# Dense-projection inputs of an attention block: fp16 parts made token-major and transposed by DMA instead of by TensorE

## Chip, cores and metric

One core of a Trainium2 chip. The metric is the device time of one execution in microseconds (us). Engines: TensorE (PE; its weight loads are PEld), VectorE (DVE), ScalarE (ACT), GpSimd (POOL), and SyncE (SP), which issues nearly all DMAs.

## What is computed

A macaron block on x of shape (2, 1024, 512), float32: half a feed-forward network (FFN), attention, half an FFN, each on a layer-normalised input and added to x.

```python
x = x + 0.5 * ffn(layernorm(x))
x = x + attn(layernorm(x))
x = x + 0.5 * ffn(layernorm(x))
# attn: q, k, v = h @ w_qkv.T + b_qkv, 32 heads of 16, 8 k/v heads, rotary, causal softmax
ctx = jnp.einsum('bhqk,bkhd->bqhd', probs, v).reshape(B, S, HIDDEN)
out = jnp.einsum('bsh,oh->bso', ctx, w_dense) + b_dense
# ffn: W = mean + mean(|w - mean|) * sign(w - mean); (silu(x @ W1.T) * (x @ W3.T)) @ W2.T
```

The change lies in `out`, the dense projection of the attention's context.

## The kernel before

All products run on PE with operands split into two fp16 parts (high and low), three products for each (`PASSES`). Tokens are 16 row tiles of 128 (8 for each of the two sequences), and tiles are grouped by four into chunks for the FFNs.

**Attention.** There are 16 groups, one for each sequence and k/v head (group g is sequence g // 8). A loop over k (PE L2058, DVE L1621) runs scores of group k for the row maxima in 25 "pieces" (`later_piece`; DVE reduces each, L1552 and L1556) beside the transposed scores and values of groups k-1 and k-2 (`scores_t` L2012, `values` L2030; exponentials on ACT, L983; masks on POOL, L734). PSUM banks are shared: a piece needs the bank of an earlier piece, given back by DVE. `split_rowmax` (L1559) ends a group; PE transposes the maxima (L2009), ACT copies them to `mrow`, and SP writes them with four DMAs (L579) into the operands of that group, which `scores_t` waits for. `transpose_context` (PE L2055) and `normalise` (DVE L1579) then write the group's context into `context`, token-major, fp32, in SBUF.

**Dense projection.** After the loop a sequence written out by hand (PE from L2148) mixes what is left of groups 14 and 15 with row tiles 0 to 7, the first sequence's, whose context is complete since group 7. For each row tile i: `transpose_rows(i)` (PE, L2124, the transposes have line L2133) makes four 128x128 fp32 transposes into PSUM bank 4 + i % 2; `context_high` (DVE L1652, from tile 8 on ACT L1035) and `context_low` (DVE L1659) write high and low fp16 parts into `ctx_t[i % 2]`; `project(i, q)` for q = 0 to 3 (PE L2136, products have line L2143) makes 12 products into the same bank; `add_dense` (DVE L1664) adds it to x. Tiles 8 to 15 follow when the attention is over: the dense tail.

**Into the second FFN.** The statistics, the normalised rows (`both_rows` L1670), their differences and their fp16 parts (`row_hi` on ACT L1041, `row_lo` on DVE L1681) of the first FFN chunk are made beside the tiles. `place_rows` (SP L594) transposes them by DMA into `xs`, two 128x1792 transposes for each of two halves (L602). `load_pair(n)` (SP L586) loads one of 28 slices of FFN weights into four slots; the first two do not overlap the attention's memory, the others do. `pair_products` (PE L2256, products have line L2271) begins the second FFN. SP works in its program's order: a wait holds all that stands behind it.

## Time and profile before

| | |
|---|---|
| median of 3 runs | 1449.14 us (1448.33 to 1449.30) |
| profiled execution | 1450.07 us, span of its profile 1448.4 us |
| PE busy | 1374.4 us, 95% of the span |
| DVE / ACT / POOL busy | 1066.3 (74%) / 608.2 (42%) / 182.7 us (13%) |
| DMA moved | 144.40 MB, mean 100 GB/s |
| chain that ended last | PE 77%, DVE 13%, SP's queue 3% |

All times of rows are microseconds from the start of the span of one profiled execution; its own time is 0.93 us above the median. A row names a line of the kernel, an engine, an operation and out<-in tiles. Matmuls are pipelined, so a busy PE is not PE at its peak. Of SP the rows show how long an issue held its queue, and the DMA view how long it took until the data landed. The granted clock of PE is given as a share of 2.4 GHz.

### The profile page before, as it was taken

The page shows a single profiled execution, that of the slowest core. Times are in us where ns is not written, and L with a number is a line of the kernel's source. Part 1 is how long each engine was busy: PE and PEld are TensorE (multiplying, and loading weights), DVE is VectorE, ACT ScalarE, POOL GpSimd, SP SyncE. Part 2 cuts the span into 40 slices and gives each one's busy share as a digit, 9 for nine tenths or more (in the row PEclk, how much of TensorE's full clock was granted, in tenths as well). Part 3 has the DMA queues.
Part 4 walks back from the last instruction along what each step waited for, and adds up shares of the span by engine and source line. Part 5 has one row for each costly group of instructions (what it writes and reads, how often), then busy time and mean ns, then how long its engine had stood idle before and what let it go on. Part 6 is the DMA issues. An engine that isn't in the chain of part 4 may idle for free.

```text
span 1448.4 us, 25511 instructions
## 1 busy us (share of the span) xinstructions
PE 1374.4 (95%) x9984; PEld 706.9 (49%) x9984; DVE 1066.3 (74%) x1611; ACT 608.2 (42%) x802; POOL 182.7 (13%) x269
## 2 busy tenths in 40 slices
PE   1999999999999978799999999999999999999998
PEld 0444444444444433233333333333577777777775
DVE  7999566764665578899999999965576666665544
ACT  4862222222211243378787777765222222222121
POOL 0000000000000354133323222211011011011000
PEclk9999999999999999699999999999999999999999
DMA  9703941011021021111111111030635646566540
GB/s 386 256 0 108 258 133 58 26 57 48 31 46 40 1 59 30 52 28 28 26 36 27 28 26 38 2 132 1 182 116 173 215 168 220 159 226 182 197 160 30
DMA packets 152028, 144.40 MB, mean 100 GB/s; under 512 B 129904, under 2 KB 133488, under 8 KB 148080
## 3 DMA queue, kind: packets, MB, share of 16 engines
q1 hardware_dynamic: 151920, 142.91, 31.4%
q8 instruction: 73, 1.20, 0.3%
q14 instruction: 35, 0.29, 0.1%
HBM read 96.73 MB, written 21.76 MB: 82 GB/s over the span
## 4 chain that ended last, share of the span: by engine, by line
PE 77%; DVE 13%; SPq 3%; issue 3%; ACT 3%; DMA 1%; POOL 0%; ACTq 0%; DVEq 0%
PE ps L2271 17%; PE ps L1819 15%; PE ps L2288 10%; PE ps L2045 9%; PE ps L1946 6%; PE ps L1840 6%; PE ps L2026 4%; PE ps L1866 3%; PE ps L2143 2%; PE ps L1936 2%; SPq L528 2%; SPq L532 2%; DVE rowmax L1552 1%; DVE w_raw L1167 1%; PE ps L2055 1%
## 5 line engine op out<-in xcount | busy, mean ns | idle before, releaser
L983 ACT ACTIVATE probs<-ps 128x1024 f32<-128x1024 f32 (+3 forms) x384 | 292.5, 812 | 83.9 <-PE ps L2026 82.3
L1819 PE MATMUL ps<-xt_hi,w_all 128*128 128x512 f16 x896 | 275.9, 382 | 16.2 <-DVE w_all L1207 16.0
L2271 PE MATMUL ps<-xs,wpair 128*128 128x256 f16 x2352 | 261.3, 273 | 0.9 <-DVE second_sum L1704 0.9
L2271 PEld LDWEIGHTS ps<-xs,wpair 128*128 128x128 f16 x2352 | 229.9, 98 | 33.7 <-DVE second_sum L1704 1.1
L1552 DVE TENSOR_REDUCE rowmax<-ps 128x2 f32<-128x1024 f32 (+3 forms) x208 | 237.3, 1141 | 9.0 <-PE ps L1954 3.8
L1946 PE MATMUL ps<-ka,qa 48*128 48x512 f16 (+3 forms) x768 | 159.7, 342 | 22.3 <-DVE rowmax L1552 9.5
L1819 PE MATMUL ps<-xt_lo,w_all 128*128 128x512 f16 x448 | 171.1, 382 | 0.0
L2045 PE MATMUL ps<-probs,vs 128*32 128x512 f32 (+3 forms) x1536 | 164.5, 500 | 2.4 <-ACT ctx_sb L1002 2.4
L1819 PEld LDWEIGHTS ps<-xt_hi,w_all 128*128 (+1 forms) x896 | 88.0, 98 | 124.9 <-issue 18.6
L1556 DVE TENSOR_REDUCE rowmax<-ps 128x1 f32<-128x512 f32 x192 | 131.1, 683 | 9.8 <-PE ps L1946 9.8
L2288 PE MATMUL ps<-wpair,hs_hi 128*128 128x512 f16 x448 | 133.4, 380 | 0.5 <-DVE hs_lo L1731 0.5
L2026 PE MATMUL ps<-qa,ka 50*128 50x512 f16 (+3 forms) x768 | 131.7, 331 | 1.7 <-DMA qa<-mrow 1.0
L1064 ACT ACTIVATE both<-both,scal 128x1024 f32<-128x1024 f32 x28 | 32.1, 1148 | 221.1 <-DVE both L1704 221.1
L734 POOL TENSOR_SCALAR_AFFINE_SELECT probs<-probs 128x512 f32<-128x512 f32 x128 | 81.2, 634 | 317.4 <-ACT probs L983 317.4
L1946 PEld LDWEIGHTS ps<-ka,qa 48*128 48x128 f16 x768 | 48.7, 95 | 139.6 <-DVE rowmax L1552 69.5
L1840 PE MATMUL ps<-w_all,hhia 128*128 (+1 forms) x336 | 100.0, 380 | 1.1 <-DVE x L1379 1.1
L1362 DVE SCALAR_TENSOR_TENSOR ha<-ps,scal,silua 128x512 f32<-128x512 f32 x42 | 31.5, 750 | 88.3 <-PE ps L1819 67.2
L2288 PE MATMUL ps<-wpair,hs_lo 128*128 128x512 f16 x224 | 85.0, 380 | 0.0
L2026 PEld LDWEIGHTS ps<-qa,ka 50*128 50x128 f16 x768 | 40.1, 94 | 67.7 <-ACT probs L983 44.5
L1819 PEld LDWEIGHTS ps<-xt_lo,w_all 128*128 (+1 forms) x448 | 44.0, 98 | 52.9 <-issue 1.1
L703 POOL TENSOR_TENSOR rot_s<-qkv_raw,sin 128x320 f32<-128x320 f32 x32 | 35.5, 1128 | 267.7 <-ACT qkv_raw L959 250.2
L910 ACT CAST hhia<-ha 128x512 f16<-128x512 f32 x42 | 25.9, 618 | 102.1 <-DVE ha L1362 102.1
(168 smaller groups left out, 1818.1 us busy)
## 6 DMA issues: line engine op xcount, KB each, us to landing
wpair<-spill SPq DMA_DIRECT2D x28, 2304.0 KB, 8.9
spill<-block_parts SPq DMA_DIRECT2D x14, 512.0 KB, 2.7
spill<-w_all SPq DMA_DIRECT2D x24, 224.0 KB, 4.0
x<-x_in SPq DMA_DIRECT2D x4, 1024.0 KB, 5.5
wbase<-m1t SPq DMA_DIRECT2D x4, 896.0 KB, 12.4
w_raw<-w1t SPq DMA_DIRECT2D x4, 896.0 KB, 13.9
wbase<-m3t SPq DMA_DIRECT2D x4, 896.0 KB, 24.0
w_raw<-w3t SPq DMA_DIRECT2D x4, 896.0 KB, 24.2
```

The lines of the kernel that those rows point to most:

```text
L734: nc.gpsimd.affine_select(out=p, in_=p, compare_op=ALU.is_ge, fill=0.0, base=0, pattern=[[0, Q_PER_KV], [1, P]], channel_multiplier=-1).th ...
L983: nc.scalar.activation(probs[u % PBUF][:, 2 * pair:2 * pair + 2, 0:q1 - q0], wide(("scores", g, (u, pair)))[:, :, 0:q1 - q0], ACT.Exp, sca ...
L1552: nc.vector.tensor_reduce(dst, src, AX.X, ALU.max).then_inc(pair_taken, 1)
L1556: nc.vector.tensor_reduce(rowmax[:, slot, kind, j:j + 1], ps[:, SINGLE_BANK, 0:w], AX.X, ALU.max)\
L1819: last = mm(ps[:, bank, :], w[a][:, k, bass.ts(t, P)], xt[b][:, k, :], start=(k == 0 and n == 0), stop=(k == HB - 1 and n == 2))
L1840: last = mm(ps[:, DOWN + j, :], hs[a][:, j * P:(j + 1) * P], w[b][:, t, :], start=(first and n == 0), stop=(last_tile and n == 2))
L1866: last = mm(ps[:, DOWN + j, :], first_split(t, a)[:, j * P:(j + 1) * P], w2s[b][:, t, :], start=(t == 0 and n == 0), stop=(t == IT - 1 and ...
L1946: return mm(ps[:, bank, off:off + w], qa[g % BUF][64 * b:64 * b + ROWS, j, qt * P:(qt + 1) * P], ka[g // 2 % BUF][64 * b:64 * b + ROWS, k0 ...
L2026: last = mm(bank[:, b, 0:q1 - q0], ka[g // 2 % BUF][64 * b:64 * b + MROWS, kt * P:(kt + 1) * P], qa[v][64 * b:64 * b + MROWS, pair, q0:q1] ...
L2045: last = mm(ps[32 * h:32 * h + 32, CTX_BANK, at:512], vs[g // 2 * 2 % BUF + h % 2][:, kt, :], probs[u % PBUF][:, h, 0:q1 - q0], start=firs ...
L2271: last = mm(product_bank(n, i)[:, m, :], weight_of(n, m, a, weight, k), xs[c % 2][:, b, 2 * rows_ + k, :], start=(k == 0 and q == 0), stop ...
L2288: last = mm(ps[:, DOWN + j, :], hs2[n % 2][a][:, q, j * P:(j + 1) * P], down_weight(n, b, q), start=(p == 0 and q == 0 and i == 0), stop=( ...
```

## The change

`transpose_rows` goes from PE. The high and low fp16 parts of the context are made token-major from `context` into three buffers `ctx_parts`, and SP transposes each part by DMA (128x512, two for each tile) into one of now four buffers `ctx_t`. The first two tiles are made inside DVE's loop over groups, in its last round. In SP's program the first two pair loads move from behind the last group's row-maximum transfers to behind those of group 14.

In order: buffers and helpers; SP (`place_context`, the loop over groups, behind it); ACT; DVE (parts, the loop over groups, behind it); PE. `project` keeps its place in PE's sequence, and the other calls of `transpose_rows` go as the last one does.

```diff
     wd_all = at("wd_all", [P, 2, HB, HID], F16, R0)
     wd = [wd_all[:, i, :, :] for i in range(2)]
     bd = at("bd", [P, HID], F32, R0 + 8192)
-    ctx_t = [[at(f"ctx_t{n}{i}", [P, HB, P], F16, R0 + 10240 + i * 2048 + j * 1024) for j, n in enumerate(("hi", "lo"))]
-             for i in range(2)]
+    ctx_t = [[at(f"ctx_t{n}{i}", [P, HB, P], F16, a + j * 1024) for j, n in enumerate(("hi", "lo"))]
+             for i, a in enumerate((R0 + 10240, R0 + 12288, D0 + 14336, C0 + 6144))]
+    ctx_parts = [at(f"ctx_parts{i}", [P, 2, HID], F16, B0 + 45056 + i * 2048) for i in range(3)]
     assert R0 + 14336 == D0
     PAIR_COLS = 2 * 3584 + 2048
...
         return {5: xt5, 6: xt6}.get(n) or (xt0 if n % 2 == 0 else xt1)
     LN_AT = {4: 4, 8: 5, 12: 6}
+    def ctx_parts_free(eng, i):
+        if i >= 3:
+            eng.wait_ge(ctx_placed[(i - 3) % 4], 32 * ((i - 3) // 4 + 1))
+    def context_rows(i):
+        return context[:, i % SEQ_TILES, :, i // SEQ_TILES, :]
+    def context_ready(eng, i):
+        b, tt = divmod(i, SEQ_TILES)
+        eng.wait_ge(single_taken, taken(("ctx", GROUPS * (b + 1) // BATCH - 1, tt // 4)))
     BLOCK_AT = {(1 if n < 8 else 2, 4 + n % 8): n for n in range(2 * HALF)}
     ON_PE = (0, 1)
...
         sp.dma_start(wd_all[:, :, :, :].rearrange("p s a b -> p (s a b)"), spill_d.ap()).then_inc(dense_loaded, 16)
         sp.dma_start(bd[:, :], b_d.partition_broadcast(P)).then_inc(dense_loaded, 16)
+        def place_context(i):
+            sp.wait_ge(ctx_hi_ready, i + 1)
+            sp.wait_ge(ctx_lo_ready, i + 1)
+            if i >= 4:
+                sp.wait_ge(dense_full, i - 3)
+            for n in range(2):
+                sp.dma_start_transpose(ctx_t[i % 4][n][:, :, :], ctx_parts[i % 3][:, n, :]).then_inc(ctx_placed[i % 4], 16)
+        def load_pair(n):
+            if n >= PAIRS:
+                return
+            if n >= WSLOTS:
+                sp.wait_ge(down2_full, n - WSLOTS + 1)
+            sp.dma_start(wpair[n % WSLOTS][:, :], image[:, n % HALF, :]).then_inc(pair_loaded[n % WSLOTS], 16)
         for g in range(GROUPS):
+            if g == GROUPS - 1:
+                place_context(0)
+                place_context(1)
             sp.wait_ge(wide_taken, drained(("rowmax", g, 0)))
             for n in range(4):
                 i, b = divmod(n, 2)
...
             if 1 <= g < GROUPS - 3:
                 sp.wait_ge(st_full, 2 * NU * g)
                 place_operands(g + 3)
-        def load_pair(n):
-            if n >= PAIRS:
-                return
-            if n >= WSLOTS:
-                sp.wait_ge(down2_full, n - WSLOTS + 1)
-            sp.dma_start(wpair[n % WSLOTS][:, :], image[:, n % HALF, :]).then_inc(pair_loaded[n % WSLOTS], 16)
+            if g == GROUPS - 2:
+                sp.wait_ge(spilled, 16 * 28)
+                for i in range(2):
+                    sp.wait_ge(blocks_spilled[i], 16 * HALF)
+                for v in range(BUF):
+                    sp.wait_ge(qk_placed[v], placed(GROUPS - BUF + v))
+                load_pair(0)
+                load_pair(1)
         def place_rows(n, j):
...
                 sp.dma_start_transpose(xs[n % 2][:, i, :, j * P:(j + 1) * P], row_parts[:, i, :])\
                     .then_inc(xs_placed[n % 2], 16)
-        sp.wait_ge(spilled, 16 * 28)
-        for i in range(2):
-            sp.wait_ge(blocks_spilled[i], 16 * HALF)
         sp.wait_ge(m_placed, 64 * GROUPS)
-        for v in range(BUF):
-            sp.wait_ge(qk_placed[v], placed(GROUPS - BUF + v))
-        load_pair(0)
-        load_pair(1)
+        for i in range(2, SEQ_TILES + 2):
+            place_context(i)
         sp.wait_ge(st_full, 2 * NU * (GROUPS - 2))
         place_rows(8, 0)
+        for i in range(SEQ_TILES + 2, SEQ_TILES + 5):
+            place_context(i)
         place_rows(8, 1)
+        for i in range(SEQ_TILES + 5, TOKEN_TILES):
+            place_context(i)
         sp.wait_ge(pv_full, NU * GROUPS)
         sp.wait_ge(single_taken, len(TURN))
         load_pair(2)
         load_pair(3)
-        sp.wait_ge(dt_full, TOKEN_TILES)
+        sp.wait_ge(dense_full, TOKEN_TILES)
         def store_rows(c):
...
         def context_high(i):
-            act.wait_ge(dt_full, i + 1)
-            act.wait_ge(dense_full, i - 1)
-            nc.scalar.copy(ctx_t[i % 2][0][:, :, :].rearrange("p a b -> p (a b)"), ps[:, rows_bank(i), :])\
+            context_ready(act, i)
+            ctx_parts_free(act, i)
+            if i == SEQ_TILES:
+                act.wait_ge(ctx_hi_ready, SEQ_TILES)
+            nc.scalar.copy(ctx_parts[i % 3][:, 0, :].rearrange("p (a b) -> p a b", a=HB), context_rows(i))\
                 .then_inc(ctx_hi_ready, 1)
         def row_hi(n, j):
...
         for i in range(SEQ_TILES, TOKEN_TILES):
             context_high(i)
-            if i in (SEQ_TILES, SEQ_TILES + 2):
-                row_hi(8, (i - SEQ_TILES) // 2)
+            if i == SEQ_TILES + 1:
+                row_hi(8, 0)
+            if i == SEQ_TILES + 4:
+                row_hi(8, 1)
         for n in range(PAIRS):
             c, p = divmod(n, HALF)
             take_first(n)
...
             if k or r >= EARLY_TAKEN:
                 reduce_piece(k, r)
+        def context_high(i):
+            context_ready(dve, i)
+            ctx_parts_free(dve, i)
+            nc.vector.tensor_copy(ctx_parts[i % 3][:, 0, :].rearrange("p (a b) -> p a b", a=HB), context_rows(i))\
+                .then_inc(ctx_hi_ready, 1)
+        def context_low(i):
+            dve.wait_ge(ctx_hi_ready, i + 1)
+            hi, lo = (ctx_parts[i % 3][:, n, :].rearrange("p (a b) -> p a b", a=HB) for n in range(2))
+            nc.vector.tensor_tensor(out=lo, in0=context_rows(i), in1=hi, op=ALU.subtract).then_inc(ctx_lo_ready, 1)
+        def context_both(i):
+            context_high(i)
+            context_low(i)
         for k in range(GROUPS):
             later_piece(k, 0)
             later_piece(k, 1)
...
             later_piece(k, 14)
             later_piece(k, 15)
             later_piece(k, 16)
+            if k == GROUPS - 1:
+                context_both(0)
             later_piece(k, 17)
             later_piece(k, 18)
             later_piece(k, 19)
             later_piece(k, 20)
+            if k == GROUPS - 1:
+                context_both(1)
             later_piece(k, 21)
             later_piece(k, 22)
             later_piece(k, 23)
...
             if ahead and p in (3, 5):
                 row_lo(9 + c, (p - 3) // 2)
-        context_high(0)
-        context_low(0)
-        context_high(1)
-        context_low(1)
+        def add_and_sum(i):
+            add_dense(i)
+            if i < TPC:
+                dve.wait_ge(x2_ready, i + 1)
+                norm_rows(8, i)
+        context_both(2)
         dve.wait_ge(wd_unit, 1)
-        add_dense(0)
-        dve.wait_ge(x2_ready, 1)
-        norm_rows(8, 0)
-        context_high(2)
-        context_low(2)
-        add_dense(1)
-        dve.wait_ge(x2_ready, 2)
-        norm_rows(8, 1)
+        add_and_sum(0)
+        context_both(3)
+        add_and_sum(1)
         normalise(14, 0)
-        context_high(3)
-        context_low(3)
-        add_dense(2)
-        dve.wait_ge(x2_ready, 3)
-        norm_rows(8, 2)
-        context_high(4)
-        context_low(4)
-        add_dense(3)
-        dve.wait_ge(x2_ready, 4)
-        norm_rows(8, 3)
+        context_both(4)
+        add_and_sum(2)
+        context_both(5)
+        add_and_sum(3)
         normalise(14, 1)
-        context_high(5)
-        context_low(5)
+        context_both(6)
         add_dense(4)
         norm_seed(8)
         norm_newton(8)
-        context_high(6)
-        context_low(6)
+        context_both(7)
         add_dense(5)
         both_rows(8, 0)
         row_differences(dve, nc.vector, 8, 0)
-        context_high(7)
-        context_low(7)
         normalise(15, 0)
         add_dense(6)
         normalise(15, 1)
         context_low(SEQ_TILES)
+        context_low(SEQ_TILES + 1)
         add_dense(7)
         row_lo(8, 0)
         for i in range(SEQ_TILES, TOKEN_TILES):
-            if i + 1 < TOKEN_TILES:
-                context_low(i + 1)
+            if i + 2 < TOKEN_TILES:
+                context_low(i + 2)
             add_dense(i)
             if i == SEQ_TILES:
                 both_rows(8, 1)
...
             later_piece(k, 24)
             values(k - 1, 4)
-        def transpose_rows(i):
-            b, tt = divmod(i, SEQ_TILES)
-            if tt % 4 == 0:
-                pe.wait_ge(single_taken, taken(("ctx", GROUPS * (b + 1) // BATCH - 1, tt // 4)))
-            if i == 0:
-                pe.wait_ge(pair_taken, NPAIR * GROUPS)
-            elif i >= 2:
-                pe.wait_ge(x2_ready, i - 1)
-            for q in range(HB):
-                last = tr(ps[:, rows_bank(i), q * P:(q + 1) * P], context[:, tt, q, b, :], ident[:, :])
-            last.then_inc(dt_full, 1)
         def project(i, q):
             if i == 0 and q == 0:
                 pe.wait_ge(dense_loaded, 32)
             if q == 0:
-                pe.wait_ge(ctx_hi_ready, i + 1)
-                pe.wait_ge(ctx_lo_ready, i + 1)
+                pe.wait_ge(ctx_placed[i % 4], 32 * (i // 4 + 1))
+                if i == 0:
+                    pe.wait_ge(pair_taken, NPAIR * GROUPS)
+                elif i >= 2:
+                    pe.wait_ge(x2_ready, i - 1)
             for n, (a, b) in enumerate(PASSES):
-                last = mm(ps[:, rows_bank(i), :], ctx_t[i % 2][a][:, q, :], wd[b][:, q, :], start=(q == 0 and n == 0),
+                last = mm(ps[:, rows_bank(i), :], ctx_t[i % 4][a][:, q, :], wd[b][:, q, :], start=(q == 0 and n == 0),
                           stop=(q == HB - 1 and n == 2))
             if q == HB - 1:
                 last.then_inc(dense_full, 1)
...
         project(7, 0)
         transpose_context(15, 1)
         project(7, 1)
-        transpose_rows(8)
         project(7, 2)
         project(7, 3)
         for i in range(SEQ_TILES, TOKEN_TILES):
-            project(i, 0)
-            if i + 1 < TOKEN_TILES:
-                transpose_rows(i + 1)
-            for q in range(1, HB):
+            for q in range(HB):
                 project(i, q)
         def pair_products(n):
```

## Rows read from the trace of the kernel before

**Rows 1.** The page: engines busy, and the granted clock of the 40 slices.
```profile
PE 1374.4 (95%) x9984; PEld 706.9 (49%) x9984; DVE 1066.3 (74%) x1611; ACT 608.2 (42%) x802; POOL 182.7 (13%) x269
...
PEclk9999999999999999699999999999999999999999
```

**Rows 2.** Windows: busy us of PE, PEld, DVE, ACT, POOL; PEclk, DMA share, GB/s.
```profile
959.00:1006.00 47.00, 46.51 (x316) 16.00 (x316) 24.17 (x52) 27.17 (x36) 6.40 (x11) 1.00 0.25 102
...
1013.00:1041.44 28.44, 25.27 (x126) 11.89 (x126) 16.86 (x24) 6.71 (x9) 0.00 (x0) 1.00 0.64 178
```

**Rows 3.** Timeline, PE, last group: start us, us, engine line op, [idle before <-releaser].
```profile
954.03 0.34 PE L1946 MATMUL ps<-ka,qa 48*128 48x384 f16 x2
```

**Rows 4.** Timeline, DVE, same stretch.
```profile
953.01 0.96 DVE L1552 TENSOR_REDUCE rowmax<-ps 128x2 f32<-128x768 f32 x1
```

**Rows 5.** Timeline, PE, first and second row transposes, first projection.
```profile
959.30 0.66 PE L2133 MATMUL ps<-ident,context 128*128 128x128 f32 x4
...
959.89 0.23 PE L2026 MATMUL ps<-qa,ka 50*128 50x128 f16 x2
...
961.56 0.59 PE L2143 MATMUL ps<-wd_all,ctx_thi 128*128 128x512 f16 x2 [0.49 <-DVE ctx_tlo L1662]
```

**Rows 6.** DVE groups by shape: count | busy us, mean ns | idle before.
```profile
L1145 DVE CAST xnorm<-xtemp 128x512 f16<-128x512 f32 x24 | 10.2, 427 | 0.8
...
L1147 DVE TENSOR_TENSOR xnorm<-xtemp,xnorm 128x512 f16<-128x512 f32 x24 | 16.6, 693 | 0.8
```

**Rows 7.** Timeline, SP: row-maximum transfers of group 14, first pair loads.
```profile
935.78 2.70 SPq L579 DMA_DIRECT2D qa<-mrow  x3
...
963.17 0.83 SPq L592 DMA_DIRECT2D wpair<-spill  x2
```

**Rows 8.** DMA issues, us to landing; second and third of windows 1000:1060, 960:985.
```profile
xt_lo<-xnorm SPq DMA_TRANSPOSE x24, 2.5
...
xs<-row_parts SPq DMA_TRANSPOSE x4, 4.3
...
wpair<-spill SPq DMA_DIRECT2D x2, 2304.0 KB, 11.5
```

**Rows 9.** Timeline, SP issues: time in which the queue is held.
```profile
514.71 1.27 SPq L499 DMA_TRANSPOSE xt_lo<-xnorm  x1
...
581.08 10.20 SPq L528 DMA_TRANSPOSE qa<-parts_q  x8
...
648.18 11.22 SPq L528 DMA_TRANSPOSE qa<-parts_q  x8
...
1016.19 3.53 SPq L602 DMA_TRANSPOSE xs<-row_parts  x2
...
1027.97 3.69 SPq L602 DMA_TRANSPOSE xs<-row_parts  x2
```

**Rows 10.** Timeline, PE, end of the attention and the dense tail.
```profile
1008.84 0.61 PE L2143 MATMUL ps<-wd_all,ctx_thi 128*128 128x512 f16 x2
...
1038.85 0.38 PE L2143 MATMUL ps<-wd_all,ctx_thi 128*128 128x512 f16 x1
...
1041.44 15.88 PE L2271 MATMUL ps<-xs,wpair 128*128 128x256 f16 x144
```

**Rows 11.** Timeline, DVE, end of the attention and the tail.
```profile
1011.07 0.42 DVE L1592 TENSOR_TENSOR context<-ps,rec 128x256 f32<-128x256 f32 x1
...
1013.16 0.75 DVE L1667 SCALAR_TENSOR_TENSOR x<-ps,scal,x 128x512 f32<-128x512 f32 x1
...
1014.07 2.03 DVE L1684 TENSOR_TENSOR row_parts<-rows,row_parts 128x1792 f16<-128x1792 f32 x1 [0.15 <-ACT row_parts L1047]
```

**Rows 12.** PE after its longest idle of the attention; windows as in rows 2.
```profile
538.54 0.61 PE L1946 MATMUL ps<-ka,qa 48*128 48x512 f16 x1 [5.02 <-DMA ka<-parts_k]
...
538.20:545.20 7.00, 6.66 (x41) 3.24 (x42) 3.74 (x5) 2.45 (x4) 2.77 (x3) 0.51 0.24 49
...
576.00:606.00 30.00, 18.77 (x130) 6.83 (x132) 24.87 (x33) 6.88 (x9) 2.30 (x6) 0.50 0.21 62
```

23 lines of the change are left out of this document (3 added, 20 removed).

## The prediction

> **What bounds the kernel now.** I read the page first: TensorE is busy for 95% of the span, at the full clock in all 40 slices but one [rows 1]. So a microsecond taken off PE's program is worth up to one microsecond, and one put in front of it costs one. The question is then what PE waits for in the three stretches that the change touches.
>
> The windows give the second reading [rows 2]. From 959 to 1006 us, where attention groups 14 and 15 are mixed with the projections of row tiles 0 to 7, PE is busy 46.5 of 47.0 us and VectorE only 24.2: there PE alone sets the pace. From 1013 to 1041.4 us, the dense tail (tiles 8 to 15), PE is busy 25.3 of 28.4.
>
> The third is the timeline of the last group of the score loop. PE starts the pair piece at 954.03 just after VectorE ends an earlier piece (953.01 + 0.96 = 953.97) [rows 3, 4]; the seven other pieces between 949 and 957 us stand the same way. So in this loop PE hands VectorE a piece at the moment at which VectorE gives a bank back. VectorE has no idle time there, and what is inserted on it moves both engines.
>
> **Part 1, transposes off PE.** One set of four holds PE from 959.30 to 959.89, 0.59 us [rows 5]. Eight such sets (tiles 0 to 7) lie in the mixed stretch; one of them took 0.49, so I take 4.6 us in all. The wait of 0.49 us ahead of the first projection [rows 5] goes too, since its tile will be ready long before. Both are on the path: -5.1 us at the end of attention. In the tail eight more sets and 3.1 us of idle time [rows 2] go, but whether this counts depends on what feeds PE there (part 3).
>
> **Part 2, two context tiles put into VectorE's last score group.** Each is a copy to fp16 (0.427 us, the nearest row is the copy of the normalised rows, same shape and same SBUF source) and a subtraction (0.693) [rows 6]. Two tiles make 2.24 us, inserted where VectorE is the tight one: +2.2 us for both engines, as rows 3 and 4 show no slack to hide it in. The lower bound is 0 (PE catches up completely), the upper 2.6 with hand-offs. The tiles 2 to 7 are copied where VectorE has half its time free [rows 2] and cost nothing; without that cover it would be 1.1 us each. ScalarE's eight copies replace eight of like size.
>
> **The moved weight loads.** The first two pair loads now start behind the row-maximum transfers of group 14, whose issues began at 935.78, so at about 938 instead of 963.17 [rows 7], and land 11.5 us after their issue [rows 8], by about 950. The first context transposes are issued at about 951, the row-maximum transfers of group 15 at about 962; neither queues behind the loads. If they did, the score rows of group 15 would wait for them. They are needed only at the start of the second FFN: 0 us. Loads two and three start after the last context transpose, seven us later than now, and are needed only when the FFN has worked off two of its 28 pairs: 0 us.
>
> **Part 3, the transposes on SP's queue.** A 128x512 transpose holds SP for 1.27 us [rows 9], and groups of eight of the operands' transposes, which are half as wide, held it for 10.20 and 11.22 us, that is 1.28 to 1.40 each. It lands 2.5 us after its issue [rows 8]. A tile needs two (high and low part): SP is held for 2.5 us, and the tile is in place 3.75 us after the first issue. In the mixed stretch eight projections fill 47 us [rows 2], one every 6 us, so this is hidden. Tile 2 stands behind the row-maximum transfers of group 15 (issued at about 962, landed by 966) and is in place by 970; projections 0 and 1 start at 961 and take until 973. If it came later, PE would wait with all of group 15 behind it, microsecond for microsecond.
>
> In the tail a projection takes PE only 1041.44 - 1038.85 = 2.59 us [rows 10], nearly the same as SP's 2.5. And in the same queue stand the two pairs of FFN row transposes, which held SP for 3.53 and 3.69 us [rows 9]. PE would be fed by SP there. Step by step, with everything at the end of attention shifted by -5.1 + 2.2 = -2.9 us:
> - Before, the projection step at 1008.84 [rows 10] was followed by the last normalisation, over at 1011.07 + 0.42 = 1011.49 [rows 11]. Now it is over at 1008.6, then comes tile 8's low part (0.69): 1009.3. PE has nothing left to project from about 1009.7.
> - SP: tiles 8 and 9 until 1014.4; the first pair of FFN rows (3.6) until 1018.0; it lands 4.3 us after its second issue [rows 8], by 1020.6, so it does not delay tile 10, which lands at +3.75, 1021.8. PE waits 3.6 us for tile 8 and 3.5 for tile 10.
> - Tile 10 is projected (2.6), VectorE adds it (0.75) and makes the second low rows (2.03) [rows 11], 0.2 for hand-offs: 1027.4. SP stood waiting for just these, with tiles 13 to 15 behind them.
> - Second pair of rows (3.65): 1031.05. Tiles 13, 14 and 15: 2.5 + 2.5 + 3.75: 1039.8, with a PE wait of 5.2 us ahead of tile 13. The last projection ends at 1042.4.
>
> Before, the FFN began at 1041.44 [rows 10]: +1.0 us. Twelve transposes of this chain at 1.35 instead of 1.25 us add 1.2, which I take because all groups of eight were slower than a single one: **+2.2 us** (bounds: +1.0, and +3.5 with each hand-off 0.1 longer).
>
> **Part 4, the clock.** PE's one long idle of the attention, 5.02 us before 538.54, was followed by the lower of the two clock levels (0.51 granted, 1.2 GHz) over the next 7 us, although PE was busy in them; and a stretch of 30 us with PE busy 63% ran at 0.50 throughout [rows 12]. The tail would have a wait of 5.2 us and be busy for 21 of 33 us. I take one fall at the wait ahead of tile 13: some 6.3 us at half speed lose 3.1 us, since PE has nothing to spare after it. Bounds: 0, and 12 for a whole tail at half speed. The last three projections would take 5.2 us each there.
>
> Sum: -5.1 + 2.2 for the attention, then the SP chain, to **+2.2** at the FFN's start, and **+3.1** for the clock: +5.3 us. The FFN behind it is bound by PE and keeps the shift. The profiled execution took 1450.07 us (span 1448.4 and 1.7 around it), 0.93 above the median; it would give 1455.4, the median 1449.14 + 5.3 = 1454.4.
>
> **Rivals.**
> - No fall of the clock, or one that SP's pace hides: +2.2, 1451.3 us (0.4 to 3.5 around it). For it: the waits of 3.5 us are followed by SP-bound tiles. Against it: [rows 12].
> - The clock falls more than once or stays low: a fall at tile 10 lengthens its projection by 2.6 us, on the chain; the whole tail low gives 8 to 12. 1457 to 1461 us. For it: the 30 us at 0.50.
> - **Faster: SP keeps ahead of PE.** If issuing a transpose cost SP little, only the first wait of 3.6 us would be left, and eight projections of 2.59: 1009.7 + 3.6 + 20.7 = 1034.0, that is -7.4 us, 1441.7. It decides at SP's share of the chain: without a fall of the clock, SP's part must be 5.1 us shorter than I have it to bring the kernel 2.9 us below the present time. Against it: every row of [rows 9]. The Trainium skill ("DMA: Bandwidth & Descriptors", section "Issuing engines are not separate DMA queues") says that a sequencer's time to initiate a DMA is usually small beside the transfer. By that rule this rival's time would come out; the trace does not agree, with 1.27 us of holding in 2.5 us to landing.
> - The change does not act, since transposes land late anyway and PE waits already in the mixed stretch: each such wait is bounded by 3.75 us; nothing in the 6 us per tile speaks for it. It lies in the slow part of the range.
>
> The skill also has a rule against this change ("VectorE: DVE Perf Modes", section "The three transpose paths"): a 128x128 transpose takes 390 ns on TensorE and 1309 ns by DMA. The trace has 0.59 us for four on PE against 3.75 for the same rows by DMA in two parts. By durations alone that is a loss for every tile; I let it stand only where PE waits, in the tail.
>
> **Numbers.** Forecast, SP chain with one fall of the clock (+3 to +7): 0.42. Without it: 0.27. Several falls: 0.15. SP ahead or a large part of VectorE's 2.2 us absorbed: 0.16. A measurement of this kernel can tell about 0.2%, 2.9 us. Faster by more than that: 0.13. Within: nearly the whole second case, the lowest of the first and some of the fourth, 0.31. Slower: 0.56. The range 1445 to 1461 leaves out most of the fast case and the end of the several falls.
>
> **What would show it.** No PE rows of the transposes, and no idle ahead of projections 0 to 7. The last score group of VectorE longer by 2.2 us. The last attention product ending about 2.9 us earlier. SP held almost without a gap from 1009 to 1038, PE waits of some 3.6, 3.5 and 5 us ahead of tiles 8, 10 and 13, released by DMA. The FFN starting near 1043 to 1047, and a granted clock under 1.00 between 1013 and 1047. The prediction is wrong if the FFN starts before 1039, if the waits sit elsewhere, or if the FFN itself changes its length, 407 us from 1041.44 to the span's end.

## The result, and the profile after

| | before | after |
|---|---|---|
| median of 20 runs | 1449.3 us | 1455.7 us |
| range | 1448.33 to 1456.88 | 1453.62 to 1457.0 |
| profiled execution (span) | 1450.07 (1448.4) | 1456.42 (1454.7) |
| second FFN begins | 1041.44 | 1047.77 |
| from there to the span's end | 407.0 | 406.9 |

The changed kernel is slower: ratio 1.0035, 95% interval 1.0027 to 1.0043, that is 3.9 to 6.2 us of 1449.3; the two medians are 6.4 us apart. The forecast was 1454.4 in a range of 1445 to 1461. All of the difference stands before the second FFN, whose length did not change.

The page of the changed kernel, engines and granted clock, answers to [rows 1]:

```profile
PE 1370.1 (94%) x9920; PEld 701.3 (48%) x9920; DVE 1063.3 (73%) x1611; ACT 607.6 (42%) x802; POOL 182.8 (13%) x269
...
PEclk8999999999999999699999999999899999999999
```

PE has 64 instructions and 4.3 us of work less, and the kernel takes longer. Two more slices now have a clock below nine tenths: the first, which lies ahead of all that was changed (it is low in some traces of unchanged code and high in others), and the one of the dense tail.

**A common zero for the traces.** Two executions of unchanged code differ by some tenths of a microsecond by the time they reach the change. One product stands ahead of everything on PE that the change moves in time, and every trace has it with the same idle ahead of it. (The moved loads are issued some 4 us before it, which is why they get an experiment of their own.) The timeline of PE has it in before and after:

```profile
942.74 0.39 PE L1946 MATMUL ps<-ka,qa 48*128 48x512 f16 x1 [0.17 <-DVE rowmax L1556]
```

```profile
942.38 0.39 PE L1982 MATMUL ps<-ka,qa 48*128 48x512 f16 x1 [0.17 <-DVE rowmax L1596]
```

I call it the marker. From it to the FFN's start it took 98.70 us before (1041.44 - 942.74) and 105.39 after, a difference of 6.69. This distance is given for every experiment below, since it leaves out what happens elsewhere in a run.

**The last score group.** PE's timeline in before and in after, at the transpose of the row maxima that ends the group:

```profile
958.91 0.24 PE L2009 MATMUL ps<-ident,nm 128*64 128x128 f16 x1
```

```profile
951.62 0.34 PE L1982 MATMUL ps<-ka,qa 48*128 48x384 f16 x2 [0.86 <-DVE rowmax L1592]
...
955.62 0.34 PE L1982 MATMUL ps<-ka,qa 48*128 48x384 f16 x2 [0.97 <-DVE rowmax L1592]
...
960.51 0.24 PE L2045 MATMUL ps<-ident,nm 128*64 128x128 f16 x1
...
962.21 0.60 PE L2170 MATMUL ps<-wd_all,ctx_thi 128*128 128x512 f16 x2
...
1005.32 0.61 PE L2170 MATMUL ps<-wd_all,ctx_thi 128*128 128x512 f16 x2
```

From the marker to that transpose it took 16.17 us before and 18.13 after: +1.96. PE waits twice for a bank, 0.86 and 0.97 us, and these answer to [rows 3, 4]. VectorE, same stretch, the first of the two tiles:

```profile
949.28 0.42 DVE L1664 CAST ctx_parts<-context 128x512 f16<-128x512 f32 x1
949.73 0.69 DVE L1670 TENSOR_TENSOR ctx_parts<-context,ctx_parts 128x512 f16<-128x512 f32 x1
```

The first projection (962.21) waits for nothing, where [rows 5] had 0.49 us. The product that answers to the 1008.84 of [rows 10] starts at 1005.32: 62.94 us from the marker instead of 66.10, that is -3.16. The last score group cost 1.96 of it, so the transposes taken off PE gave 5.12.

**The tail.** PE's waits there, and the start of the FFN:

```profile
1012.43 1.03 PE L2170 MATMUL ps<-wd_all,ctx_thi 128*128 128x512 f16 x2 [3.25 <-DMA ctx_tlo<-ctx_parts]
...
1021.96 0.74 PE L2170 MATMUL ps<-wd_all,ctx_thi 128*128 128x512 f16 x2 [2.69 <-DMA ctx_tlo<-ctx_parts]
...
1037.30 1.03 PE L2170 MATMUL ps<-wd_all,ctx_thi 128*128 128x512 f16 x2 [5.71 <-DMA ctx_tlo<-ctx_parts]
...
1047.77 12.50 PE L2286 MATMUL ps<-xs,wpair 128*128 128x256 f16 x113
```

SP's timeline over the same stretch: both parts of tile 8, the first pair of row transposes, the low parts of tiles 10 and 12, the second pair of row transposes, and the low part of tile 13 (answers to [rows 9]):

```profile
1008.65 1.19 SPq L598 DMA_TRANSPOSE ctx_thi<-ctx_parts  x1
1009.88 1.27 SPq L598 DMA_TRANSPOSE ctx_tlo<-ctx_parts  x1
...
1013.87 3.51 SPq L639 DMA_TRANSPOSE xs<-row_parts  x2
...
1019.44 1.27 SPq L598 DMA_TRANSPOSE ctx_tlo<-ctx_parts  x1
...
1024.68 1.27 SPq L598 DMA_TRANSPOSE ctx_tlo<-ctx_parts  x1
1029.21 3.50 SPq L639 DMA_TRANSPOSE xs<-row_parts  x2
...
1034.77 1.27 SPq L598 DMA_TRANSPOSE ctx_tlo<-ctx_parts  x1
```

Each wait of PE ends 2.5 us after the low part of its tile was issued (1009.88 to 1012.43, 1019.44 to 1021.96, 1034.77 to 1037.30). From 1025.95 (1024.68 + 1.27) to 1029.21 SP stands idle: it waits for the second low rows, and the transposes of tiles 13 to 15 stand behind them. VectorE shows why these rows come late, since they follow the addition of tile 10 (answers to [rows 11]):

```profile
1026.45 0.75 DVE L1714 SCALAR_TENSOR_TENSOR x<-ps,scal,x 128x512 f32<-128x512 f32 x1 [4.62 <-PE ps L2170]
1027.12 2.02 DVE L1731 TENSOR_TENSOR row_parts<-rows,row_parts 128x1792 f16<-128x1792 f32 x1
```

Tile 10 kept PE from 1021.96 to the addition at 1026.45, 4.5 us where the prediction had 2.6. The windows of the same execution (busy us of PE, PEld, DVE, ACT, POOL; PEclk, DMA share, GB/s) give the reason:

```profile
1012.10:1015.50 3.40, 3.07 (x8) 1.13 (x9) 0.40 (x1) 1.06 (x2) 0.00 (x0) 0.50 0.51 103
1022.30:1025.70 3.40, 3.40 (x10) 1.22 (x8) 0.00 (x0) 0.93 (x2) 0.00 (x0) 0.50 0.49 99
1036.00:1042.80 6.80, 5.50 (x13) 1.94 (x14) 0.16 (x1) 0.00 (x0) 0.00 (x0) 0.50 0.66 98
```

The clock fell to its lower level (0.50 granted, 1.2 GHz) at all three waits: 0.4 us before the end of the wait ahead of tile 8, 0.3 us into tile 10, and 1.3 us before the end of the wait ahead of tile 13. The first fall is hidden: tiles 8 and 9 run slowly while SP is behind anyway. The second delays the addition of tile 10, and with it SP. The third makes the last three projections take 10.47 us (1037.30 to 1047.77) instead of the 7.8 of full speed.

### The profile page after: what moved, and what is told of

It reads as the page before. It is cut to its first block, busy times and chain, and to the rows that moved or that the text cites. A ratio compares the mean times of both kernels' runs of the same rounds, so it can differ in the third digit from the quotient of the medians.

```text
span 1454.7 us, 25424 instructions
## 1 busy us (share of the span) xinstructions
PE 1370.1 (94%) x9920; PEld 701.3 (48%) x9920; DVE 1063.3 (73%) x1611; ACT 607.6 (42%) x802; POOL 182.8 (13%) x269
## 4 chain that ended last, share of the span: by engine, by line
PE 76%; DVE 13%; issue 3%; SPq 3%; ACT 3%; DMA 1%; POOL 0%; ACTq 0%; DVEq 0%
PE ps L2286 17%; PE ps L1855 14%; PE ps L2303 10%; PE ps L2081 9%; PE ps L1982 6%; PE ps L1876 6%; PE ps L2062 5%; PE ps L1902 3%; PE ps L2170 2%; DVE rowmax L1592 2%; PE ps L1972 2%; PE ps L2091 1%; DVE w_raw L1207 1%; DVE rowmax L1596 1%; SPq L545 1%
```

## Experiments

Theory: SP's queue sets the tail, issue after issue, and the falls of the clock in PE's waits come on top; the two tiles in VectorE's last score group cost about 2 us on the path; the moved pair loads cost nothing. Rivals: the moved loads or what queues behind them; the row transposes in the queue rather than the number of issues; the work given to VectorE in the tail. Here is what all kernels gave. The ratio is to the kernel before, run beside each of them (its medians were 1449.2 to 1449.5). Times and distances do not carry the same weight: the distance is one execution of each kernel, and the intervals of waits_filled, second_rows_last and pair_on_gpsimd overlap that of the changed kernel, so that for these three a gain over the changed kernel rests on the distance and on the medians, and is not clear of the noise by the ratio.

| kernel | median us (runs) | ratio (95%) | marker to FFN |
|---|---|---|---|
| before | 1449.3 (20) | | 98.70 |
| after | 1455.7 (20) | 1.0035 (1.0027 to 1.0043) | 105.39 |
| loads_moved | 1450.02 (10) | 1.0002 (0.9992 to 1.0012) | 98.70 |
| loads_back | 1463.78 (4) | 1.0102 (1.0085 to 1.0119) | 112.22 |
| waits_filled | 1453.63 (6) | 1.0029 (1.0016 to 1.0041) | 101.42 |
| second_rows_last | 1453.29 (7) | 1.0037 (1.0020 to 1.0054) | 100.62 |
| pair_behind_loop | 1457.46 (4) | 1.0070 (1.0047 to 1.0092) | 103.56 |
| pair_on_gpsimd | 1453.88 (6) | 1.0025 (1.0013 to 1.0038) | 103.48 |
| rows_out_of_tail | 1445.90 (11) | 0.9978 (0.9969 to 0.9988) | 94.69 |
| rows_and_pair | 1443.43 (5) | 0.9958 (0.9944 to 0.9972) | 92.31 |
| one_transpose | 1450.30 (10) | 0.9997 (0.9984 to 1.0011) | 99.65 |
| all_three | 1438.76 (5) | 0.9929 (0.9915 to 0.9942) | 88.23 |

### The pair loads

**loads_moved**: the kernel before, with nothing but the move of the first two pair loads.

```diff
         for g in range(GROUPS):
...
                 place_operands(g + 3)
+            if g == GROUPS - 2:
+                sp.wait_ge(spilled, 16 * 28)
...
+                load_pair(0)
+                load_pair(1)
...
         sp.wait_ge(m_placed, 64 * GROUPS)
...
-        load_pair(0)
-        load_pair(1)
         sp.wait_ge(st_full, 2 * NU * (GROUPS - 2))
```

> The kernel before with one part of the change alone: the first two pair loads issued behind the row-maximum transfers of group 14. Theory (SP's queue feeds the dense tail): the loads cost and bring nothing, 1449.3 us, FFN start within 0.5 us of 1041.4. Rival (the early loads disturb attention's last group through the DMA engines): 1 to 3 us slower, with longer waits of PE or SP between 938 and 960 us.

The distance from the marker to the FFN is the one of before to the hundredth, 98.70. The move alone costs nothing and brings nothing.

**loads_back**: the changed kernel, with the two loads where they stood before, so that the transposes of tiles 2 to 9 are issued behind them.

```diff
         sp.wait_ge(m_placed, 64 * GROUPS)
...
+        load_pair(0)
+        load_pair(1)
         for i in range(2, SEQ_TILES + 2):
             place_context(i)
```

> The changed kernel with the first two pair loads back behind the row-maximum transfers of group 15. Theory: the transposes of tiles 2 and on then stand behind 4.6 MB of loads; they land 10 to 12 us later, at about 978 instead of 970, and PE waits for tile 2 (3 to 6 us) if the DMA engines serve SP's queue in order: 1459 to 1461 us. Rival (the loads are the harm of the change): the attention gets faster than in the changed kernel, 1453 us or less.

SP's timeline behind the loads, then PE's:

```profile
965.47 0.83 SPq L606 DMA_DIRECT2D wpair<-spill  x2
966.41 1.31 SPq L598 DMA_TRANSPOSE ctx_thi<-ctx_parts  x1
967.76 1.29 SPq L598 DMA_TRANSPOSE ctx_tlo<-ctx_parts  x1
969.16 7.54 SPq L598 DMA_TRANSPOSE ctx_thi<-ctx_parts  x1
976.76 2.41 SPq L598 DMA_TRANSPOSE ctx_tlo<-ctx_parts  x1
```

```profile
980.34 1.04 PE L2169 MATMUL ps<-wd_all,ctx_thi 128*128 128x512 f16 x2 [6.96 <-DMA ctx_tlo<-ctx_parts]
```

Two transposes behind the loads are issued at the usual pace; the third holds SP for 7.54 us and the fourth for 2.41, until the second load is in (issued at 965.9, landed 13.3 us later). PE then waits 6.96 us in the middle of the attention, and the FFN starts 6.83 us later than in the changed kernel (112.22 against 105.39). The direction was as expected and the size above it. So the move of the loads is needed with this change, and it is what keeps it from costing 14 us.

### What the clock costs

**waits_filled**: the changed kernel; PE makes 12, 10 and 20 products into a free bank ahead of tiles 8, 10 and 13. They are added to the work, and their results go nowhere.

```diff
+        pe.wait_ge(wide_taken, len(WIDE))
         for i in range(SEQ_TILES, TOKEN_TILES):
+            for n in range({SEQ_TILES: 12, SEQ_TILES + 2: 10, SEQ_TILES + 5: 20}.get(i, 0)):
+                mm(ps[:, 2, :], ident16[:, :], wd[0][:, 0, :], start=True, stop=True)
```

> The changed kernel with PE kept busy in its three waits of the tail by products whose result nobody reads: 12 ahead of tile 8, 10 ahead of tile 10, 20 ahead of tile 13 (of 0.216 us each, less than the waits of 3.25, 2.69 and 5.71 us). It computes the same result. Theory: the clock stays at 1.00 in the tail, the projection of tile 10 takes 2.6 us instead of 4.3 and tiles 13 to 15 7.8 instead of 10.5: FFN start 4.4 us earlier, at about 1043.4, 1451.3 us. Rival (the waits alone make the loss, the clock only follows): same time as the changed kernel within 1 us.

PE's timeline in the tail, and the window over it:

```profile
1008.24 2.75 PE L2270 MATMUL ps<-wd_all,ident 128*128 128x512 f16 x12
...
1016.86 2.32 PE L2270 MATMUL ps<-wd_all,ident 128*128 128x512 f16 x10
...
1029.03 4.48 PE L2270 MATMUL ps<-wd_all,ident 128*128 128x512 f16 x20
...
1035.22 0.61 PE L2170 MATMUL ps<-wd_all,ctx_thi 128*128 128x512 f16 x2 [1.71 <-DMA ctx_tlo<-ctx_parts]
...
1043.04 15.23 PE L2289 MATMUL ps<-xs,wpair 128*128 128x256 f16 x138
```

```profile
1008.24:1043.04 34.80, 30.45 (x140) 12.85 (x139) 15.90 (x23) 4.95 (x7) 0.00 (x0) 1.00 0.67 139
```

No fall is left, and with work that serves nothing this execution is shorter. The distance is 101.42: 3.97 us less than in the changed kernel and 2.72 more than before. That parts the loss in two. The SP chain without any fall of the clock costs +2.7; the falls cost 4.0, of which 1.7 on SP's chain (the second rows are issued 85.10 us after the marker instead of 86.83) and 2.65 on the last three projections (7.82 instead of 10.47), less 0.4 that the second row transposes held SP longer. In the medians the gain is smaller, 2.1 us (1455.7 to 1453.63), with the six runs from 1451.46 to 1455.4; by the two ratios it is 0.9 us, inside the noise. Each run's mean granted clock is on record: 0.987 in the two shortest, 1451.46 and 1451.67, and 0.980 to 0.985 in the other four, so the clock may have fallen somewhere in these all the same. One profile can't say where. The clock's part is 4 us in the profiled pair and some 2 us, or less, over the runs.

### The row transposes in SP's queue

**second_rows_last**: only SP's order is changed; the second row transposes go behind tile 15.

```diff
         place_rows(8, 0)
-        for i in range(SEQ_TILES + 2, SEQ_TILES + 5):
+        for i in range(SEQ_TILES + 2, TOKEN_TILES):
             place_context(i)
         place_rows(8, 1)
-        for i in range(SEQ_TILES + 5, TOKEN_TILES):
-            place_context(i)
```

> The changed kernel with the second pair of FFN row transposes issued behind tile 15 instead of between tiles 12 and 13. Theory (tiles 13 to 15 wait in SP's queue behind these rows, which wait for tile 10): the wait ahead of tile 13 goes, SP ends tile 15 at about 1034, the rows land at about 1040.5, and the FFN starts there: 7 us faster than the changed kernel, 1448.5 us. Rival (VectorE's added copies and the first two waits make the loss): the wait only moves to another tile, less than 2 us faster.

SP's timeline, VectorE's, and PE's at the start of the FFN:

```profile
1024.22 1.27 SPq L598 DMA_TRANSPOSE ctx_tlo<-ctx_parts  x1
1027.65 1.19 SPq L598 DMA_TRANSPOSE ctx_thi<-ctx_parts  x1
```

```profile
1024.97 2.02 DVE L1729 TENSOR_TENSOR row_parts<-rows,row_parts 128x1792 f16<-128x1792 f32 x1
1026.91 0.68 DVE L1668 TENSOR_TENSOR ctx_parts<-context,ctx_parts 128x512 f16<-128x512 f32 x1
```

```profile
1042.55 15.88 PE L2284 MATMUL ps<-xs,wpair 128*128 128x256 f16 x144 [1.06 <-DMA xs<-row_parts]
```

The rows no longer hold tile 13 in the queue, but its low part is made behind the low rows on VectorE, so SP stands idle all the same from 1025.49 to 1027.65. The distance is 100.62. Against the kernel with filled waits, the fair comparison since here too no fall delays the end, the new order is worth only 0.8 us in the distance, and the ratio shows no gain (1.0037). The expectation of 7 us was missed, and its rival, that the wait only moves to another tile, came nearer (PE waits 1.89 us ahead of tile 13 and 1.94 ahead of tile 15): two queues, VectorE's and SP's, held tile 13, and I had taken it out of one. The row transposes, now last, cost PE time in two ways: the low part of tile 15, with them right behind it in the queue, takes 4.6 us from issue to landing instead of 2.5, and the FFN's start waits 1.06 us for them.

This trace also says something of the clock. Up to tile 12 it runs the same program as the changed kernel, with the same wait of 3.25 us ahead of tile 8; but the clock fell only 1.1 us into that tile (0.50 from 1013.1 to 1016.5) and did not fall at all behind the wait of 2.48 us ahead of tile 10, where the changed kernel lost 1.7 us behind 2.69. So how much the falls cost differs from one execution to the next.

**rows_out_of_tail**: the statistics come right behind tile 3, and the first rows, with their transposes, inside the attention. Tile 8 is made on VectorE right behind its normalisation, the high part of the first rows moves from ScalarE to VectorE, and the second rows come last. The diff shows SP and the core of VectorE.

```diff
-        for i in range(2, SEQ_TILES + 2):
+        for i in range(2, SEQ_TILES):
             place_context(i)
...
         place_rows(8, 0)
-        for i in range(SEQ_TILES + 2, SEQ_TILES + 5):
+        for i in range(SEQ_TILES, TOKEN_TILES):
             place_context(i)
         place_rows(8, 1)
-        for i in range(SEQ_TILES + 5, TOKEN_TILES):
-            place_context(i)
...
         add_and_sum(3)
+        norm_seed(8)
+        norm_newton(8)
...
         normalise(15, 0)
+        context_both(SEQ_TILES)
         add_dense(6)
...
             if i == SEQ_TILES:
-                both_rows(8, 1)
-                row_differences(dve, nc.vector, 8, 1)
-            if i == SEQ_TILES + 2:
                 row_lo(8, 1)
```

> The changed kernel with SP's tail left to the context tiles: statistics of the first FFN chunk right behind tile 3, first row parts made and transposed inside the attention, second row transposes behind tile 15, and tile 8 made by VectorE alone right behind the normalisation it needs. Theory (SP's chain sets the tail): tile 8 in place at about 1010.1, tiles 2.6 us apart, last projection over at 1031, row transposes landed at 1033.6, where the FFN starts: 14 us faster than the changed kernel, 1441.5 us, and 8 faster than the kernel before. Rival (the DMA transposes are slower than PE's in themselves, whatever else is in the queue): the tiles come more than 3.4 us apart, as before the change, and the FFN starts later than 1040.

The median is 1445.9, 3.2 us under the kernel before by the ratio, and the distance 94.69, 10.7 less than in the changed kernel. The profiled execution itself was 1452.61, the highest of the eleven: the clock had fallen at 850.3 us, to 0.50 until 857.1, long before this stretch, which the distance from the marker leaves out. PE's waits are 1.02 to 1.59 us each, and the clock does not fall in the tail. The order of nearly the same work, with as many transposes, was worth more than the whole loss. It came out some 4 us above what was expected: all of PE's waits ahead of a tile are still released by the transpose of a low part, and the FFN's first product waits 1.32 us for the row transposes. The kernel rows_and_pair below has the same order, and its trace shows what holds the low parts: SP stands idle from 1010.02 to 1011.55 and from 1014.06 to 1015.33, until VectorE, busy with the second rows, has made them (1010.80 + 0.69 and 1014.58 + 0.69).

### The pair in the last score group

**pair_behind_loop**: tiles 0 and 1 are made behind VectorE's loop instead of in it.

```diff
             later_piece(k, 16)
-            if k == GROUPS - 1:
-                context_both(0)
...
+        context_both(0)
+        context_both(1)
         context_both(2)
```

> The changed kernel with the parts of tiles 0 and 1 made by VectorE behind its loop over groups instead of inside its last round. Theory (2.0 us of copies stand on the path inside the loop): the last row-maximum transpose of PE comes 2.0 us earlier (at about 958.5 instead of 960.5), without the waits of 0.86 and 0.97 us on VectorE; but tile 0 is in place only at about 962.7, PE waits 2.5 us for it, and the FFN starts 0 to 1 us later than in the changed kernel: 1456.0 us. Rival (PE has slack for the pair in the loop): the transpose stays near 960.5 and the wait for tile 0 is added in full, 1458 us.

PE's timeline:

```profile
958.50 0.24 PE L2043 MATMUL ps<-ident,nm 128*64 128x128 f16 x1
...
963.11 0.59 PE L2168 MATMUL ps<-wd_all,ctx_thi 128*128 128x512 f16 x2 [2.85 <-issue]
```

The transpose of the maxima is 16.17 us behind the marker (958.50 - 942.33), as before the change: the pair accounts for the 1.96 us, all of it. But now PE waits 2.85 us for tile 0, and the product that answers to 1005.32 starts 63.88 us behind the marker, 0.94 later than in the changed kernel, as expected. The distance to the FFN is 1.83 shorter all the same: in this execution, the shortest of the four, the clock stayed low longer in tiles 8 to 10 (0.50 from 1012.5 to 1019.4) and did not fall at tile 10, which PE then waited for only 1.19 us. The four runs lie between 1454.52 and 1463.37, so the time says little more than that the place is no better.

**pair_on_gpsimd**: the same two tiles on GpSimd, which has nothing to do for 8 us there.

```diff
         for k in range(GROUPS + 2):
...
+            if k == GROUPS - 1:
+                context_pair(0)
+                context_pair(1)
...
             later_piece(k, 16)
-            if k == GROUPS - 1:
-                context_both(0)
```

> The changed kernel with the parts of tiles 0 and 1 made by GpSimd in a stretch where it idles for 8 us (after 938 us). Theory: VectorE's last round is 2.0 us shorter, nothing waits for tile 0, and the whole rest moves by 2.0 us: FFN start 1045.8, 1453.7 us. Rival (GpSimd's copies from SBUF slow VectorE or delay the masks): less than 1 us gained.

GpSimd's timeline, first tile, and PE's:

```profile
937.04 0.61 POOL L781 CAST ctx_parts<-context 128x512 f16<-128x512 f32 x1
937.73 1.16 POOL L783 TENSOR_TENSOR ctx_parts<-context,ctx_parts 128x512 f16<-128x512 f32 x1
```

```profile
957.67 0.24 PE L2054 MATMUL ps<-ident,nm 128*64 128x128 f16 x1
```

Again 16.17 us behind the marker (957.67 - 941.50), and no wait for tile 0. The distance falls by 1.91 and the median by 1.8 (the ratio by 1.4 us, with overlapping intervals): VectorE's 1.96 us, passed on to the end as expected. GpSimd needs 0.61 and 1.16 us where VectorE needs 0.42 and 0.69, which costs nothing since nobody waits for it.

**rows_and_pair**: the last two kernels together (rows_out_of_tail with tiles 0 and 1 on GpSimd).

```diff
             place_context(i)
...
+            if k == GROUPS - 1:
+                context_pair(0)
+                context_pair(1)
```

> The two together (row transposes out of the tail, and tiles 0 and 1 on GpSimd). Theory: both gains add, since they lie on the path one behind the other: FFN start at 1031.6, 1439.5 us. Rival: the shorter attention leaves VectorE too little time for the row parts and tile 8, so that less than 1 us of GpSimd's 2 is left.

1443.43 us, 2.5 under rows_out_of_tail, and the distance is 2.38 less. The two gains add. The time expected, 1439.5, was missed by the same 4 us as in rows_out_of_tail.

### The number of issues

**one_transpose**: the changed kernel, with one transpose of 1024 columns for each tile instead of two of 512. Bytes and order are as they were; the buffers of a tile's two parts become one tile, and the waits count one transfer instead of two.

```diff
-            for n in range(2):
-                sp.dma_start_transpose(ctx_t[i % 4][n][:, :, :], ctx_parts[i % 3][:, n, :]).then_inc(ctx_placed[i % 4], 16)
+            sp.dma_start_transpose(ctx_both[i % 4][:, :, :, :].rearrange("p n q c -> p (n q) c"),
+                                   ctx_parts[i % 3][:, :, :].rearrange("p n h -> p (n h)")).then_inc(ctx_placed[i % 4], 16)
```

> The changed kernel with one DMA transpose of 128x1024 for each context tile instead of two of 128x512, into the same place. Theory (SP's time for each issue, not the moving of the data, sets the pace): the issue holds SP for 1.3 to 1.75 us, between the rows for 512 and for 1792 columns, instead of 2.5 for the two; tile 10 lands 2 to 2.5 us earlier, the first row transposes then wait for VectorE, and the FFN starts at about 1045 instead of 1047.8: 1452.8 us. Rival (the transfer itself is the cost): one issue of 1024 columns holds SP as long as two of 512 and lands no earlier: same time as the changed kernel within 1 us.

All issues of one line, in the changed kernel and in this one (min/median/max ns that an issue held the queue), and the time to landing:

```profile
L598 SPq DMA_TRANSPOSE ctx_thi<-ctx_parts x16: 1189/1199/1911, 950.5 to 1038.8; - x16
L598 SPq DMA_TRANSPOSE ctx_tlo<-ctx_parts x16: 1198/1267/2283, 951.8 to 1040.0; - x16
```

```profile
L597 SPq DMA_TRANSPOSE ctx_t<-ctx_parts x16: 1232/1244/2077, 949.7 to 1031.3; - x16
...
DMA to landing us min/median/max: 3.0/3.1/4.4
```

This is the clearest of the experiments. A transpose of 1024 columns holds SP for 1.24 us, one of 512 for 1.20 to 1.27. Between these two sizes the cost is that of the issue, not of the columns (the row transposes, with 1792 columns, hold it for 1.75 each). A tile takes SP 1.25 us instead of 2.5 and is in place 3.1 us after its issue instead of 3.75. The changed kernel with this one edit is level with the kernel before (0.9997, 0.9984 to 1.0011), 5.4 us under the changed kernel; the distance is 5.74 less. It was better than expected, because the wait ahead of tile 10 shrank to 0.16 us and there was no fall of the clock there; the falls at tiles 8 and 13 remain (0.50 at 1012 to 1014 and at 1032 to 1035). As second_rows_last shows, the fall at tile 10 can be missing by chance too, so some of the 5.74 may be luck.

**all_three**: rows_and_pair with one transpose for each tile. The low parts are made three tiles ahead, and the second rows are placed behind tile 13.

```diff
         place_rows(8, 0)
-        for i in range(SEQ_TILES, TOKEN_TILES):
+        for i in range(SEQ_TILES, SEQ_TILES + 6):
             place_context(i)
         place_rows(8, 1)
+        for i in range(SEQ_TILES + 6, TOKEN_TILES):
+            place_context(i)
...
-            if i + 2 < TOKEN_TILES:
-                context_low(i + 2)
+            if i + 3 < TOKEN_TILES:
+                context_low(i + 3)
```

> Row transposes out of the tail, tiles 0 and 1 on GpSimd, one transpose for each tile; in addition the context parts are made three tiles ahead on VectorE and the second row transposes stand behind tile 13. Theory: tile 8 lands at about 1008, PE then has a tile at hand every 2.6 us, and the FFN starts at 1029 to 1030 instead of 1035.1 in the kernel with the first two edits: 1437.5 us, 12 us faster than the kernel before. Rival (another wait takes the place: VectorE's order or the row transposes in the queue hold back tile 14): 1440 us or more, with one PE wait of over 2 us in the tail.

PE's timeline of the whole tail, and its window:

```profile
1006.64 7.94 PE L2179 MATMUL ps<-wd_all,ctx_t 128*128 128x512 f16 x36 [0.34 <-DMA ctx_t<-ctx_parts]
1014.77 7.93 PE L2179 MATMUL ps<-wd_all,ctx_t 128*128 128x512 f16 x36 [0.19 <-DVE x L1719]
1024.51 5.35 PE L2179 MATMUL ps<-wd_all,ctx_t 128*128 128x512 f16 x24 [1.80 <-DMA ctx_t<-ctx_parts]
1029.70 15.88 PE L2295 MATMUL ps<-xs,wpair 128*128 128x256 f16 x144
```

```profile
1006.64:1029.70 23.06, 21.07 (x97) 9.20 (x98) 12.89 (x20) 4.58 (x6) 0.00 (x0) 1.00 0.84 195
```

Eight projections in 23.1 us, at full clock, with 2.0 us of waits among them (23.06 - 21.07) and 0.34 us ahead of them. The time is 1438.76 us (1438.6 to 1439.13), ratio 0.9929 (0.9915 to 0.9942): 10.4 us under the kernel before by the medians beside it (1449.19), and some 16 under the changed one (15.4 by the two ratios, 16.9 by the medians). It beats both, and is 1.3 us above the 1437.5 expected. What is left is the 1.80 us ahead of tile 14, which stands behind the second row transposes.

## Why the prediction was right, point by point

**Attention.** The transposes off PE were put at -5.1 and gave -5.12; the pair on VectorE at +2.2 and cost +1.96; the end of the attention at -2.9 and came -3.16. Both experiments that took the pair out of the loop gave the 1.96 back at the transpose of the maxima. The moved loads were put at 0, and loads_moved measured 0.

**SP's chain.** The waits ahead of tiles 8, 10 and 13 were put at 3.6, 3.5 and 5.2 us, released by DMA, and were 3.25, 2.69 and 5.71. (The 3.6 is a slip: the prediction's own 1009.3 + 3.75 - 1009.7 makes 3.35.) Tile 10 was forecast in place at 1021.8 and was so at 1021.96; its wait is shorter because the low clock stretched tiles 8 and 9 into it. The chain was forecast to move the FFN's start by +2.2 without any fall of the clock. waits_filled, with no fall, has +2.72. The mechanism was right, with small misses in it. Measured from the marker, tile 8 was in place 0.3 us before the forecast and tile 10 0.5 us after it. The surcharge of 1.2 us, for twelve issues at 1.35, stands for two things in the trace: from issue to issue the transposes took 1.31 us each, 2.62 a tile (1020.82 to 1023.44), where the plain sum has 2.5; and the first transpose behind each pair of row transposes held SP for 1.90 us (1017.50) and 1.91 (1032.81), which no term of the sum had.

**The clock: the term that was mis-sized.** "I take one fall at the wait ahead of tile 13: some 6.3 us at half speed lose 3.1 us". There were three falls. The one named lasted 6.8 us in the window shown but cost 2.65, since it began 1.3 us before PE's wait was over. A second, at tile 10, cost 1.7 on the chain: the rival of several falls had put 2.6 there, for a whole projection at half speed, while the clock came back within the tile. Less the 0.4 that the second row transposes held SP longer, 4.0 against 3.1. The first fall was hidden behind SP. So three falls did not make the 1457 to 1461 us that this rival gave; the forecast case and its rival were less far apart than I had them. That the second fall came at all is in part chance: second_rows_last and loads_back, which run the same program there, did not have it behind waits of 2.48 and 2.51 us. This is why the FFN began at 1047.77, a little above the 1043 to 1047 named.

**The rivals.** That SP keeps ahead is excluded by the holds of 1.20 and 1.27 us in 2.5 us to landing, and confirmed as the deciding point from the other side: half the issues, and 5.4 us of the loss are gone. That nothing acts because transposes land late in the mixed stretch was wrong: PE's timeline has no wait of a projection from tile 0 to 7 in it. By the Trainium skill ("DMA: Bandwidth & Descriptors", section "Issuing engines are not separate DMA queues") the sequencer's time for a DMA is usually small beside the transfer; here it was half of the time to landing (1.20 and 1.27 us in 2.5), and one_transpose shows that it is paid for each instruction.

**The transpose itself.** The Trainium skill ("VectorE: DVE Perf Modes", section "The three transpose paths") has 390 ns on TensorE against 1309 ns by DMA for one 128x128 block in bf16. The trace has 0.59 us for four fp32 blocks on PE, less a block than the page. In one_transpose eight blocks land 3.1 us after one issue, 0.39 us a block, though in a pipeline and not alone. By durations alone the DMA path looked like a loss for every tile; with one issue a tile, fed early enough, all_three is 10.4 us under the kernel whose transposes are on PE.

**What stays open.** How much of the 6 us the clock takes at the median: 4.0 in the profiled pair, 2.1 in the medians of waits_filled, 0.9 in its ratio. Why pair_behind_loop scatters by 9 us was not tried. The new order of the rows was not tried in the kernel before, so its share of all_three's 10.4 us is not parted from that of the transposes; as an estimate it could bring that kernel at most 3.2 us, since its tail has no more idle time ([rows 2]: 28.44 - 25.27). Nor were the early low parts and the new place of the second rows in all_three tried by themselves.

## What to carry to other kernels

When work moves from the bounding engine to DMA, write down the issuing queue as an engine of its own: so many issues at so many microseconds, in program order, with everything that an issue waits for. Here two issues a tile, 2.6 us from one tile to the next, stood against 2.6 us of PE's work, and one merged instruction for each tile turned the loss into a draw. Then look at what in that queue waits for somebody else, and put it behind what the bounding engine needs next, on the producing engine as well as in the queue. Work added beside a tight loop belongs on an engine that is idle there, even one that takes half as long again for it (1.77 us a tile on GpSimd, 1.11 on VectorE).

## What the runs showed of the hardware

- An issue of a transpose held SP for 1.20 to 1.27 us with 512 columns, for 1.24 with 1024 and for 1.75 with 1792. To landing it took 2.5, 3.1 and 4.3 us. The first transpose of 512 columns close behind a pair of 1792 held SP for 1.90 us (1017.50 in the changed kernel). With such a pair right behind it, the low part of tile 15 took 4.6 us to landing in second_rows_last and 4.0 in rows_and_pair.
- Two transposes could be issued behind two large pair loads at the usual pace; the third held SP for 7.54 us and the fourth for 2.41 (loads_back). In pair_on_gpsimd the same stood at 7.41 and 2.37, harmless there, since nothing behind them was urgent.
- PE's clock fell to 1.2 GHz beside the waits of 3.25, 2.69 and 5.71 us in the changed kernel, of 3.25, 2.59 and 5.67 in pair_on_gpsimd, and of 3.25 and 3.38 in one_transpose. It stayed at 2.4 GHz behind waits of 2.85 us (pair_behind_loop, 963.11), 2.51 (loads_back, 1029.84) and 2.48 (second_rows_last), and in all of the tail of rows_and_pair, whose waits were at most 1.46. Yet it fell once in rows_out_of_tail, at 850.3, beside a wait of 1.07 us. The length of the last wait alone does not tell whether a fall comes.
- With products that serve nothing in the waits the clock stayed at 2.4 GHz in the tail, and the distance was 3.97 us shorter than with the waits left idle; over the runs the gain was 2.1 us at the median and not clear of the noise by the ratio.
